# Where seven waiting tiles are copied home: four of the copies move from VectorE to GpSimd

## The reference, cut to what matters

```python
qkv = (x @ w_qkv).reshape(b, n, 3, H, hd).transpose(2, 0, 3, 1, 4)
attn = jnp.einsum('bhnd,bhmd->bhnm', q, k) * scale
attn = jnp.where(attn_mask[None, None] == 0, -jnp.inf, attn)
attn = jax.nn.softmax(attn, axis=-1)
o = jnp.einsum('bhnm,bhmd->bhnd', attn, v).transpose(0, 2, 1, 3).reshape(b, n, d)
o = o @ w_proj + b_proj
ln = (o - mu) * jax.lax.rsqrt(var + LN_EPS) * ln_gamma + ln_beta
x = _layernorm(x + o + ln, axis=-1)
```

## Time and profile before

| | |
|---|---|
| median of 3 runs | 3217.51 us (3217.07 to 3221.09) |
| the profiled execution's own time | 3214.41 us |
| its span in the profile | 3212.6 us |
| mean granted TensorE clock | 0.983 of full |
| busy share of the span: PE, ACT, POOL, DVE | 94%, 82%, 78%, 77% |

### The profile page before, as it was taken

One profiled execution on the slowest core, in us unless ns is written; L12 is line 12 of the kernel. 1 busy time (PEld: TensorE's weight loads), 2 busy tenths in 40 slices (PEclk: granted clock), 3 DMA queues, 4 the chain that ended last, 5 costly groups with the idle time before them and its releaser, 6 DMA issues.

```text
span 3212.6 us, 121377 instructions
## 1 busy us (share of the span) xinstructions
PE 3035.8 (94%) x42504; PEld 1892.9 (59%) x42504; DVE 2481.6 (77%) x4601; ACT 2621.1 (82%) x3849; POOL 2500.2 (78%) x1543
## 2 busy tenths in 40 slices
PE   6989999999999999999999999999999999999984
PEld 3656656656665656656566666656656566665552
DVE  5567777878778787787878878787787877878775
ACT  5888888888888888888888888888888888888871
POOL 2777878787887878888787887878878788887883
PEclk9999999999999999999999999999999999999997
DMA  7999999999999999999999999999999999999993
GB/s 208 192 190 199 208 198 211 199 211 205 206 212 197 214 202 206 213 199 211 200 210 205 207 211 197 215 201 206 214 199 208 199 210 206 207 212 187 202 197 97
DMA packets 2187078, 648.05 MB, mean 202 GB/s; under 512 B 2135408, under 2 KB 2135408, under 8 KB 2186992
## 3 DMA queue, kind: packets, MB, share of 16 engines
q1 hardware_dynamic: 2133808, 548.28, 93.1%
q10 hardware_dynamic: 53184, 98.59, 9.3%
HBM read 76.28 MB, written 33.55 MB: 34 GB/s over the span
## 4 chain that ended last, share of the span: by engine, by line
POOL 45%; issue 31%; PE 10%; SPq 7%; DMA 2%; DVE 2%; ACT 1%; POOLq 1%; DVEq 0%; ACTq 0%
POOL p_split L780 37%; SPq L309 7%; POOL x_res L796 4%; PE scores_a L411 3%; PE side L375 2%; DMA pt<-p_split 2%; POOL norm L804 2%; POOL norm L799 2%; PE side L357 2%; PE proj L392 1%; PE pv_bank L432 1%; PE pv_bank L434 1%; PE pv_bank L433 1%; POOL shift L807 1%; POOLq L779 1%
## 5 line engine op out<-in xcount | busy, mean ns | idle before, releaser
L780 POOL TENSOR_TENSOR p_split<-p,p_split 128x1024 f16<-128x1024 f32 x1024 | 2178.6, 2144 | 642.8 <-ACT p_split L517 641.1
L504 ACT ACTIVATE p<-p,row_min 128x1024 f32<-128x1024 f32 x1024 | 1170.7, 1144 | 279.0 <-DVE row_min L662 277.1
L517 ACT ACTIVATE p_split<-p 128x1024 f16<-128x1024 f32 x1024 | 1047.2, 1046 | 120.4 <-DMA pt<-p_split 119.9
L432 PE MATMUL pv_bank<-v_both,pt 128*128 128x64 f16 x8192 | 830.5, 193 | 39.2 <-DMA pt<-p_split 31.2
L662 DVE CUSTOM_DVE_ANT_0 p<-scores_a,mask_q 128x1024 f32<-128x1024 f32 x512 | 626.2, 1223 | 309.4 <-PE scores_b L411 259.9
L434 PE MATMUL pv_bank<-v_both,pt 128*128 128x64 f16 x8192 | 831.4, 194 | 0.0
L433 PE MATMUL pv_bank<-v_both,pt 128*128 128x64 f16 x8192 | 831.3, 194 | 0.0
L432 PEld LDWEIGHTS pv_bank<-v_both,pt 128*128 128x128 f16 x8192 | 741.0, 98 | 126.5 <-issue 62.1
L433 PEld LDWEIGHTS pv_bank<-v_both,pt 128*128 128x128 f16 x8192 | 730.6, 98 | 67.9 <-issue 1.6
L434 PEld LDWEIGHTS pv_bank<-v_both,pt 128*128 128x128 f16 x8192 | 731.4, 98 | 0.0
L375 PE MATMUL side<-xt,w_hi 128*128 128x512 f16 x2048 | 636.0, 382 | 7.8 <-DVE q_lo L641 7.2
(11 more groups left out here) (80 smaller groups left out, 4411.2 us busy)
## 6 DMA issues: line engine op xcount, KB each, us to landing
x_in<-in_x ACTq DMA_DIRECT2D x60, 512.0 KB, 5.3
x_res<-in_x ACTq DMA_DIRECT2D x120, 256.0 KB, 3.5
out<-x_res ACTq DMA_DIRECT2D x120, 256.0 KB, 3.3
pt<-p_split SPq DMA_TRANSPOSE x1024, 4.9
pt<-in_adj SPq DMA_DIRECT2D x8, 512.0 KB, 10.0
ot<-in_L_gnn_w_qkv SPq DMA_DIRECT2D x4, 768.0 KB, 9.7
p<-in_x SPq DMA_DIRECT2D x8, 256.0 KB, 5.0
p<-in_x ACTq DMA_DIRECT2D x8, 256.0 KB, 8.5
```

The source lines that it names most:

```text
L432: nc.tensor.matmul(o, hi, v_hi, start=(kt == 0 and at == 0), stop=False, skip_group_check=True)
L504: nc.scalar.activation(p32[:, slot, :], p32[:, slot, :], ACT.Exp, bias=row_min[:, slot:slot + 1], scale=-1.0, accum_out=row_sum[:, head:he ...
L517: nc.scalar.activation(p_split[:, head % RING, HI, :], p32[:, head % RING, :], ACT.Copy).then_inc(hi_done, 1)
L780: nc.gpsimd.tensor_tensor(p_split[:, slot, LO, :], p32[:, slot, :], p_split[:, slot, HI, :], ALU.subtract).then_inc(lo_done, 1)
```

## The change

`COPY`, the slot of each copy, becomes [12, 13, 15, 16, 13, 15, 17]. The copies of tiles 0 to 3 are issued by GpSimd in slots 12, 13, 15 and 16, those of tiles 4 to 6 by VectorE in slots 13, 15 and 17: all of these slots held copies before. In a slot POOL's copy stands behind its `low_part` and ahead of the addition of beta. The waits for V1 and X0 stand ahead of the first copy of each of the two engines. Copy 3 on POOL raises `x_copied[0]`, copy 6 on DVE raises `x_copied[1]`. Nothing else changes.

```diff
-COPY = [12, 13, 13, 15, 16, 17, 17]
+COPY = [12, 13, 15, 16, 13, 15, 17]
...
             def copy_tile(g, t):
 
-                if t == 0:
+                if t == 4:
                     wait_alone(dve, side_ready, side_done(g, "V1"))
                     wait_alone(dve, side_dve, side_done(g, "X0"))
...
-                if t in (3, 6):
-                    move.then_inc(x_copied[t // 4], 1)
+                if t == 6:
+                    move.then_inc(x_copied[1], 1)
...
-                    for t in range(7):
+                    for t in range(4, 7):
                         if COPY[t] == s:
                             at_end(dve, g, lambda: copy_tile(g, t))
...
+            def copy_tile(g, t):
+
+                if t == 0:
+                    wait_alone(pool, side_ready, side_done(g, "V1"))
+                    wait_alone(pool, side_dve, side_done(g, "X0"))
+                move = nc.gpsimd.tensor_copy(xt[:, place(t), :, :, :].rearrange("p h k n -> p (h k n)"),
+                                             xt[:, waiting(t // 2, t % 2), :, :, :].rearrange("p h k n -> p (h k n)"))
+                if t == 3:
+                    move.then_inc(x_copied[0], 1)
+
             def body(g):
                 for s in range(SLOTS):
                     u, j = s // QUARTERS, s % QUARTERS
                     if j % 2 == 0:
                         low_part(g, u, j // 2)
+                    for t in range(4):
+                        if COPY[t] == s:
+                            at_end(pool, g, lambda: copy_tile(g, t))
                     if s in (14, 30):
```

## The result

The changed kernel takes 3271.91 us by its median (3269.61 to 3272.59), the kernel before 3217.29 beside it (3216.53 to 3221.09): the ratio is 1.0166, with a 95% interval of 1.0148 to 1.0184. That is 55 us slower, where 59 were forecast (3276, range 3240 to 3325). The profiled execution took 3272.15 us, its span is 3270.3, 57.7 more than before.

What follows compares the result with a forecast made beforehand. PE bounds ordinary groups; groups with copies cost 4.9 us extra. Q0 6.9 us late plus 2.0 for the clock makes 8.9, so 4.0 more in each of 15 groups, 60 us: 3276 us stated, range 3240 to 3325.

Steps and rivals of the forecast that it cites:

- The gate: Q0 on PE waits for copy 3 in POOL's queue: copy done at 798.5, Q0 at 798.6, 6.9 us late, PE idle 6.0.
- The copy's price: One tile copy on POOL takes 1.1 us, bounded by 0.5 and 2.14, and counts four times ahead of Q0.
- VectorE's relief: With fewer DVE copies, unit 4's scores are 0.85 us late instead of 3.06; alone it saves 3 to 4 us a group.
- The half clock: After the idle wait at Q0, PE runs at half clock, losing 2.0 us a group with nothing covering it; bounds 0 and 3.
- The sum: A group with copies costs 8.9 us over an ordinary one, before 4.9: 4.0 us more, 60 us in 15 groups.
- What is late next: POOL's late LO halves and the DMA's pause cost nothing behind PE's delay; without this cover, up to 1 us a group.
- A: Rival: DVE's relief is the whole effect and Q0's wait is satisfied in time; 54 us less, 3164 us; chance 0.06.
- B: Rival: no measurable change, POOL's copy at 0.5 to 0.7 us, clock kept in most groups; about 3217 us; chance 0.05.
- C: Rival: GpSimd copies as slowly as it subtracts, near 2 us a copy; 114 us more, 3331 us; chance 0.12.

## Why the prediction was right, step by step

To compare, 795.10 - 785.90 = 9.20 us is taken off the times of the changed kernel, so that both groups have unit 2's head a start on POOL at 785.90.

- **The gate (right).** Copy 3's end was forecast at 798.5 and came at 807.21 - 9.20 = 798.0. Q0 was forecast for 798.6 and began at 798.4: 0.35 us passed between the copy's end and Q0, not the 0.1 allowed. The wait is 5.83 us where 6.0 stood. Three runs (the wait removed, copy 3 one instruction sooner, the owners swapped) show that it is this wait and the place in the queue, not GpSimd's work.
- **The copy's price (right).** 1.1 us taken, 1.04 us measured as the median; the mean over 60 is 1.14, because some include a wait for VectorE's copy. The doubled copies show the factor four, as 3.83 us for four more. That a copy would follow GpSimd's memset and one-element rows was a bet: nothing in the trace before excluded a price near that of the subtraction.
- **VectorE's relief (right).** Unit 4's scores were forecast 0.85 us late and are 0.81 us late (798.81 - 9.20 against 788.80), with PE idle for 0.71 ahead of them. The run without GpSimd copies prices this side alone at 70 us (3215.48 to 3145.04), 63 of them in the 15 groups; the change gave that back, and 55 us more, at Q0.
- **The half clock (mechanism right, size slightly too small).** 2.0 us taken. In the group shown it is 813.59 - 807.56 = 6.03 us from Q0 to unit 5's scores, against 3.39 at full clock: 2.64 lost. Over the 15 groups the mean is 2.25, and keeping PE busy gives back 2.3 a group. The two groups of 55.01 us have only 3.41 us of half clock and lose about 1.3. The prediction halved a whole half-clock stretch; here a part of the stretch lies inside the idle time, where it costs nothing (next section).
- **The sum.** Forecast 8.9 us over an ordinary group; the 13 groups between the first and the last average 8.9, the group shown has 9.3. That the average fits so closely is in part luck: Q0 is 6.7 us late instead of 6.9 (798.36 against 791.68), and the clock takes 2.3 in these groups instead of 2.0. All 15 gave 56 us instead of 60. Multiplying one group by 15 was the rough step: the first and the last such group rose by only 2.5 and 2.9 us against before, the 13 others by 3.9 on average.
- **What is late next (right under its cover).** With PE waiting, no late LO half showed. With the wait removed it costs 0.4 us a group at unit 6's scores, and 0.5 us more near the group's end whose origin is open: within the "up to 1 us" that was given.
- **The rivals.** A needed Q0's wait to be satisfied in time; the trace has it 15 times. B and C needed a copy near 0.6 or 2 us. By the Trainium skill ("GPSIMD Engine Reference", section on elementwise cycle accounting) the port-bound loop would give 0.9 us and the tight software loop 1.5, both estimates from its cycles an element. The measured 1.04 us stands near the first and speaks against the second for this copy.

## What to carry to other kernels

Before work moves to another engine, find its first reader, and sum what stands ahead of it in the new engine's queue up to the last piece that the reader waits for: here that sum, not the engine's busy share of 78%, set the result. A VectorE copy that met a GpSimd subtraction cost up to 2.2 us here instead of 0.42; put it where the other engine waits for something anyway. Give the early-read part to the engine that is quick and early, the late-read part to the slow one.

## What the runs showed of the hardware that was not expected

- The half clock's cost hardly follows the idle time ahead of it: 1.64 us lost after 3.76 us idle, 2.0 to 2.9 (in two groups 1.3) after 5.83, and 5.84 - 3.39 = 2.45 in the group shown after 9.66. What it follows is how much of the half-clock stretch lies behind Q0's start. The stretches around Q0 with copy 3 sooner, then with the copies doubled; columns as in the earlier trace rows:

```profile
797.63:801.03 3.40, 3.40 (x31) 1.98 (x29) 0.99 (x5) 0.00 (x0) 3.40 (x3) 0.50 0.52 99
815.36:825.59 10.23, 5.09 (x33) 2.63 (x34) 0.20 (x2) 1.04 (x2) 8.96 (x6) 0.50 0.63 120
```

In the first, all 3.40 us lie behind Q0's start (796.31), and half of that is 1.7, with 1.64 lost. After the change 813.04 - 807.56 = 5.48 us do, half 2.74, with 2.64 lost. With the copies doubled 825.59 - 820.50 = 5.09 us do, half 2.55, with 2.45 lost. In the kernel before, after 2.97 to 4.53 us idle, the clock fell in 11 of the 15 groups and stayed full in the others, one of them after 3.41 us.

- A conditional on TensorE in front of a wait left it idle for 0.27 us even when the branch wasn't taken; the ordinary groups grew from 47.1 to 47.4 us.
- When GpSimd has instructions waiting in a row, a blocked VectorE copy gets in between two of them: it then costs VectorE up to the rest of one subtraction (copies of 2.15 and 2.20 us in the rows above, up to 2.38 before) and GpSimd 0.15 to 0.27 us (two copies in 2.23 us, one in 1.31, where 1.04 is usual).
